# A graph network's segment sums: three written-out tiles per half and a loop of tile pairs, in place of two and a loop of single tiles

## What is computed

```
x = layernorm(x + SAGE(x))     3 layers: mean of x[src] at dst, @ Wl + bl + x @ Wr, relu between
x = layernorm(x + GIN(x))      gelu(x[src] + edge_attr @ bond_W + bond_b) * edge_weight1, summed at dst; two dense layers
x = layernorm(x + GCN(x))      2 layers: (x @ W)[src] scaled by degrees and edge_weight, summed at dst; relu, layer norm
x = layernorm(x + RGCN(x))     2 layers: h_rel[edge_type, src] summed at dst, + h @ loop_w + b
```

## Time and profile before

| what | value |
|---|---|
| median of 3 runs | 6518.18 us (6513.54 to 6526.69) |
| profiled execution | 6529.06 us |
| its span, first to last instruction | 6527.2 us |
| mean granted clock of PE | 0.864 of 2.4 GHz |
| busy: PE, DVE, ACT, POOL | 4735.7, 3273.3, 2416.2, 1918.4 us |
| chain that ended last | PE 22%, DVE 8%, issue 7%, ACT 4% of the span |

### The profile page before, as it was taken

One profiled execution on the slowest core, in us unless ns is written; L12 is line 12 of the kernel. 1 busy time (PEld: TensorE's weight loads), 2 busy tenths in 40 slices (PEclk: granted clock), 3 DMA queues, 4 the chain that ended last, 5 costly groups with the idle time before them and its releaser, 6 DMA issues. The chain is left out here.

```text
span 6527.2 us, 120714 instructions
## 1 busy us (share of the span) xinstructions
PE 4735.7 (73%) x23954; PEld 3001.6 (46%) x23955; DVE 3273.3 (50%) x10024; ACT 2416.2 (37%) x4967; POOL 1918.4 (29%) x1886
## 2 busy tenths in 40 slices
PE   5887677566868888756665776775888876777776
PEld 3553443233335555344442443433666644656552
DVE  4443343456444454456664666664444433555564
ACT  2342332344247776345542444442222221222222
POOL 5531760643033331064402433102223202222210
PEclk9998899788779999877787778887999998888887
DMA  4552663454234443244432444332333322333322
GB/s 132 176 167 95 203 204 123 143 163 155 84 95 143 142 145 126 86 135 138 135 114 78 142 133 133 124 111 73 112 102 103 108 96 80 96 92 98 92 82 83
DMA packets 429789, 789.70 MB, mean 121 GB/s; under 512 B 69303, under 2 KB 75250, under 8 KB 429716
## 3 DMA queue, kind: packets, MB, share of 16 engines
q1 hardware_dynamic: 375060, 671.58, 30.8%
q0 software_dynamic: 54656, 117.32, 7.4%
HBM read 480.10 MB, written 308.53 MB: 121 GB/s over the span
## 5 line engine op out<-in xcount | busy, mean ns | idle before, releaser
L1033 PE MATMUL p_agg<-onehot,msg 128*128 128x512 f16 (+1 forms) x2384 | 1046.1, 439 | 1028.6 <-DVE onehot L1430 624.0
L627 POOL DMA_INDIRECT raw<-node_s,src_i x980 | 962.1, 982 | 2036.3 <-DMA node_s<-o 855.5
L1430 DVE TENSOR_SCALAR onehot<-iota,dst_f,negbase 128x512 f16<-128x512 f16 (+1 forms) x2384 | 970.8, 443 | 972.8 <-PE p_agg L1035 470.7
L1035 PE MATMUL p_agg<-onehot,msg 128*128 128x512 f16 (+1 forms) x2384 | 1055.6, 443 | 0.0
L1033 PEld LDWEIGHTS p_agg<-onehot,msg 128*128 x2384 | 240.5, 101 | 1533.3 <-issue 1470.0
L1421 DVE TENSOR_TENSOR msg<-raw,msg x140 | 180.4, 1289 | 685.1 <-ACT msg L748 643.4
L1479 DVE BATCH_NORM_STATS2 stats<-v_ring 128x6 f32 (+1 forms) x1960 | 426.9, 281 | 187.0 <-ACT v_ring L826 135.1
L627 POOL DMA_INDIRECT raw<-node_x,src_i x392 | 379.4, 968 | 458.0 <-issue 445.4
L818 ACT ACTIVATE o<-v_ring,nmr,rstd 128x128 f32 (+1 forms) x1176 | 472.2, 483 | 101.5 <-DVE nmr L1495 95.1
L1408 DVE SCALAR_TENSOR_TENSOR hid<-type_in,p_wide 128x512 f32<-128x512 f32 x448 | 251.1, 616 | 321.1 <-PE p_wide L1013 235.3
L788 ACT ACTIVATE u<-p_agg,sage_bias 128x512 f32<-128x512 f32 x196 | 133.9, 683 | 703.8 <-PE p_agg L1064 703.4
(11 more groups left out here) (252 smaller groups left out, 7977.2 us busy)
## 6 DMA issues: line engine op xcount, KB each, us to landing
node_s<-o SPq DMA_DIRECT2D x392, 256.0 KB
feature<-u SPq DMA_DIRECT2D x294, 256.0 KB, 2.1
h_in<-feature SPq DMA_DIRECT2D x294, 256.0 KB
node_x<-o SPq DMA_DIRECT2D x294, 256.0 KB
res_in<-node_x SPq DMA_DIRECT2D x294, 256.0 KB, 3.2
h_in<-node_x SPq DMA_DIRECT2D x196, 256.0 KB
h_in<-node_s SPq DMA_DIRECT2D x196, 256.0 KB
h_t<-dinv_scratch SPq DMA_DIRECT2D x196, 256.0 KB, 3.8
```

Source lines behind the costliest of these rows:

```text
L627: nc.gpsimd.indirect_dma_start(out=raw[:, (e % RING) * BATCH + j, :], out_offset=None, in_=src_d, in_offset=bass.IndirectOffsetOnAxis(ap=s ...
L1033: nc.tensor.matmul(p_agg[:, a, :], tile_ap(msg, t, 0, D), oh, start=first, stop=True, skip_group_check=True)
L1035: return nc.tensor.matmul(p_agg[:, a, :], tile_ap(msg, t, D, 2 * D), oh, start=False, stop=True, skip_group_check=True)
L1430: return V.tensor_scalar(tile_ap(onehot, slot), iota[:, :], dst_f[:, bass.ds(t, 1)], negbase[:, bass.ds(it * 2 + a, 1)], ALU.subtract, ALU ...
```

## The change

`EVERY` becomes 3, so each half has three written tiles, needed or not. A turn of the loop takes `GROUP` = 2 tiles, with one wait and one signal for both, from a ring of two groups (four places). The setup counts turns of two, moves a first tile down where the last turn would pass tile 195 (with these edges no first tile moves), and has six more linked instructions.

```
-EVERY = 2
+EVERY = 3
+GROUP = 2
 MORE = 2
+GROUPS = -(-TILES // GROUP)
...
-        onehot = sb("onehot", [P, 2 * EVERY + MORE, HALF], F16)
+        onehot = sb("onehot", [P, 2 * EVERY + MORE * GROUP, HALF], F16)
...
-        def tile_of(t0, i0, i):
-            return (t0 + (i - i0) + EVERY).with_bounds(min_val=0, max_val=TILES - 1)
+        def tile_of(t0, i0, i, j):
+            return (t0 + (i - i0) * GROUP + (EVERY + j)).with_bounds(min_val=0, max_val=TILES - 1)
...
-            return ((i % MORE) + 2 * EVERY).with_bounds(min_val=2 * EVERY, max_val=2 * EVERY + MORE - 1)
+            return ((i % MORE) * GROUP + (2 * EVERY + j)).with_bounds(
+                min_val=2 * EVERY, max_val=2 * EVERY + MORE * GROUP - 1)
...
                             wait_apart(pe, rounds_s.oh_ready, i + 1)
-                            item(a, tile_of(t0, i0, i), ring_place(i), False).then_inc(rounds_s.oh_used, 1)
+                            for j in range(GROUP):
+                                last = item(a, tile_of(t0, i0, i, j), ring_place(i, j), False)
+                            last.then_inc(rounds_s.oh_used, 1)
...
-            link(V.scalar_tensor_tensor(out=n_items[g, :], in0=last1, scalar=float(-EVERY), in1=first,
+            link(V.scalar_tensor_tensor(out=some, in0=last1, scalar=float(-EVERY), in1=first,
                                         op0=ALU.add, op1=ALU.subtract))
+            link(V.tensor_scalar(o[g, 1, 0:GROUPS], colf[g, 0:GROUPS], float(GROUP), some, ALU.mult, ALU.is_lt))
+            link(V.tensor_reduce(n_items[g, :], o[g, 1, 0:GROUPS], AX.X, ALU.add))
+            link(V.tensor_scalar(some, n_items[g, :], float(-GROUP), float(TILES - EVERY), ALU.mult, ALU.add))
+            link(V.tensor_tensor(first, first, some, ALU.min))
+            link(V.tensor_scalar(last1, n_items[g, :], float(GROUP), float(EVERY), ALU.mult, ALU.add))
+            link(V.tensor_tensor(last1, last1, first, ALU.add))
...
                             dve.wait_ge(rounds_s.oh_used, i + 1)
-                            compare(ring_place(i), tile_of(t0, i0, i)).then_inc(rounds_s.oh_ready, 1)
+                            for j in range(GROUP):
+                                last = compare(ring_place(i, j), tile_of(t0, i0, i, j))
+                            last.then_inc(rounds_s.oh_ready, 1)
```

More of the change, by code:

```diff
@@ L370, in items_of, with ring_place @@
             return t0.with_bounds(min_val=0, max_val=TILES - EVERY), i0, i1
-        def tile_of(t0, i0, i):
-            return (t0 + (i - i0) + EVERY).with_bounds(min_val=0, max_val=TILES - 1)
-        def ring_place(i):
-            return ((i % MORE) + 2 * EVERY).with_bounds(min_val=2 * EVERY, max_val=2 * EVERY + MORE - 1)
+        def tile_of(t0, i0, i, j):
+            return (t0 + (i - i0) * GROUP + (EVERY + j)).with_bounds(min_val=0, max_val=TILES - 1)
+        def ring_place(i, j):
+            return ((i % MORE) * GROUP + (2 * EVERY + j)).with_bounds(
+                min_val=2 * EVERY, max_val=2 * EVERY + MORE * GROUP - 1)
         def each_batch(eng, e0, e1, body):
```

## The result

The changed kernel takes **6364.23 us** (median of 4 runs, 6357.67 to 6366.91), the kernel before beside it 6522.43. The ratio is 0.9756, 95% interval 0.9743 to 0.977: 2.4% faster, 158 us, and outside the range of 6445 to 6590. The profiled execution took 6366.74 us, its span is 6364.5.

What follows compares the result with a forecast made beforehand. PE was taken as busiest in every round but nowhere full, with 0.64 of tile work on the path. The terms, 139 - 63 - 127 + 50 + 1 = 0, gave 6518 us, no change, range 6445 to 6590.

Steps and rivals of the forecast that it cites:

- Counts, gap and setup: Signs: tile matmuls and compare each x2848; 0.56 us "issue" gap in every loop turn; setup +1 us.
- C: Longer halves of a round: single-tile loop turns become fewer two-tile turns of 1.75 us, -127 us (-158 to +19).
- Term E: Setup: six more linked DVE instructions at some 0.2 us each ahead of the list, +1 us.
- What would show it: Expected trace signs: two-tile turns 1.75 us apart, 21-tile half 18 us, last eight halves shorter, clock 0.85 to 0.88.
- rival 3: Faster by the clock: more matmuls per half raise PE's mean granted clock by 0.02, -61 us, 6457 us; chance 0.10.
- A: Third written tile on PE in the 384 halves with no turn: +139 us (bounds +68 and +227).
- D: DVE's flag to PE comes 0.32 us later, after three compares instead of two: +50 us (bounds 0 and 96).
- B: The 272 halves with one turn: their tile is now written out, saving loop overhead, -63 us (bounds -29 and -98).
- Rival 1: Slower: the third tile and later flag lie on the PE-DVE-ACT circle's path, +75 us, 6593 us; chance 0.28.
- rival 4: The two-tile loop turn saves nothing at 2.37 us, sum +146, 6664 us; two compares could leave PE waiting; chance 0.04.
- Rival 2: Faster: PE's waits for DVE swallow the added tile, share 0.3 everywhere, -72 us, 6446 us; chance 0.24.

Runs made afterwards that it cites:

- run 3: The kernel before with MORE = 4 in place of 2 (ring of four one-hots, still two written tiles and single turns): 6424.7 us, ratio 0.9865.
- run 5: The changed kernel with MORE = 1, a ring of one group (two places): 6789.85 us against 6756.4 for the kernel before on a slower chip, ratio 1.006.
- run 11: The kernel before with one more matmul, of zeros, in each loop turn: 6693.29 us against 6756.4 for the kernel before on a slower chip, ratio 0.9918.
- run 6: The changed kernel with PE leaving out the third written tile's matmuls, DVE still making its one-hot (sums wrong): 6265.12 us, ratio 0.9617.
- run 7: The changed kernel with DVE leaving out the third written compare, PE multiplying the second one-hot twice (sums wrong): 6238.29 us, ratio 0.9567.
- run 8: The changed kernel with DVE signalling after the second compare and again after the third, in all rounds: 6339.8 us, ratio 0.9725.

## Why the prediction was wrong

**Counts, gap and setup: right.** L1036, L1038 and the compare stand at x2848. The gap is there once per turn, 0.56 us, so the row was the figure to go by. The Trainium skill's smaller one (Advanced Engine Details and Errata, Control Flow Timing) would have made C even smaller. Term E was +1; the first matmul of L1036 is 1.5 us later.

**"What would show it": half wrong.** The turn of two was to be 1.75 us and is 1.59, the 21-tile half 18 and is 14.6. Each round's last eight halves are shorter, by 22 to 35 us, and RGCN 1's halves of 3.6 us take 4.0, both as said. SAGE 0, GIN and RGCN 1 were to move least and moved by 23, 41 and 25 us; the GCN rounds were to move by less than 10 us, and GCN 1 moved by 22. RGCN 1's first 82 halves together changed by under 1 us. The clock, at 0.884, left its band of 0.85 to 0.88.

**Term C is the step that failed**: "the 15 longer halves", forecast -127 us, measured -255. The half with 19 turns was priced at 6.3 us less at full clock and takes 9.1 less, those with three turns at 1.4 and take 2.3 less. Of the 255 us, 204 lie between a half's first matmul and the nodes' own part, and 51 in what comes behind. Three things were missing in it.

- *The ring.* The prediction priced turns and never the places, and read no row of DVE's waits behind PE. Two more places are worth 88 us by themselves (run 3) and 51 to 95 of the 255 in the last 16 halves; taking them back from the change costs 162 there (run 5). They let PE run through tiles that wait for it, and let DVE leave the loop sooner.
- *The turn.* 1.75 us was taken, 1.62 called the least; it is 1.59. Over the 15 turns a round behind the halves' first ones that is 0.16 x 120, some 20 us.
- *The clock.* C was mixed 73 to 27 from full and half clock, both held as they were. But with the denser loop the clock of these halves rose, and with work put into the single-tile loop's gaps it rose too (run 11). What that gave in time was not measured. In the longest half it is little: GCN 1's had full clock before and is 7.6 us shorter all the same.

The clock's mean rose by 0.02, which was **rival 3** (chance 0.10, 61 us). It was right in the clock's direction, and its "against" was wrong: it looked at PE's waits for DVE in short halves, where the clock moved little (SAGE 2 0.78 and 0.77), and not at the loop's own gaps. It was also set up as another case beside C, while both come from the same denser loop. Its 61 us are neither shown nor refuted.

**A, the third tile on PE**: forecast +139 for the halves without a turn. The work was priced rightly: from first matmul to the nodes' own part they take 212 us more, and 227 was the forecast. The share was not: leaving the tile out gives 91 us over all halves, and in those without a turn the trace is only 48 us shorter (run 6), below A's lower bound of 68. The shares were off by round: GCN 2 0.3 us, RGCN 1 33, SAGE 2 33 of 707.

**D, DVE's later flag**: forecast +50, bounds 0 and 96. Compare and flag together measure 123 us (run 7), 67 of them in GCN 2. That is more than the upper bound, but not all of it is D: in halves with a turn the kernel before made this compare too, in its loop. In those without one it is 67 us by the traces, above the forecast and inside the bounds. There, and in GCN 2 above all, the compare's own time is on DVE's path, and the prediction counted only the flag's delay, because "a loop compare already ran there": true for halves with a turn, not for the 48 without. The flag alone is worth 20 us (run 8).

**A, B and D together**: forecast +126. Shared out by halves (D's 50 over all 784), that is +164 for those without a turn, measured +126, and -46 for those with one, measured -35. The sum was near by errors that cancel, which is luck: A too high, D too low. B by itself wasn't isolated.

**Rival 1** (6593), which wanted over 0.85 of the added work on the path, and **rival 4** (the pair saves nothing) are refuted for this kernel: 212 us of added tile work made 126 of time, DVE's part included, a share of 0.6. Run 5 shows the ground of rival 4's last sentence: with one group PE does wait for two compares, 2.52 us a turn. **Rival 2** (6446) was nearest, for another reason than its own.

What stays open: how the 80 to 118 us of the pairs divide between saved gaps and clock, as no run held the clock fixed; why RGCN 1 lost 17 us with the flag in all rounds and gained 13 with it in the SAGE rounds alone; and what the slower chips' "remote" waits are.

## What to carry to other kernels

Before pricing a loop's turn, look at both engines of the ring: rows "consumer waits for producer" and "producer waits for consumer". If the producer waits (471 us here), depth is a lever by itself (88 us here); and the grouped turn paid here only with two groups. Where gaps in a loop lie between matmuls, read the granted clock along one long loop, for a change that closes gaps can raise it. What the clock is worth is then read from the time between turns at both levels (1.18 and 1.22 us here), not from PE's busy time, since at half clock the matmuls stretch into the gaps. A unit of work written out "always" is to be priced in each stage on the engine that bounds that stage: here it was free on PE and 67 us on DVE in GCN 2, and 33 us on PE and free on DVE in RGCN 1.

## What the runs showed that was not expected

- A matmul of zeros in each turn of the loop made the kernel before 0.8% faster (ratio 0.9918), with the clock of the last 16 halves of SAGE 2 at 0.95 in place of 0.70.
- The same loop turn is 1.12 us with three matmuls and 1.18 with two, at full clock.
- A turn of one tile takes 1.18 us at full clock and 1.22 at half, SAGE 2 aside, so a clock at half level costs this loop's turns next to nothing.
- The kernel before took 3.6% and 4.7% longer (6756 and 6824 in place of 6520 us) on two chips than on the others. For the one kernel traced on both kinds all of it lies outside the last 16 halves of the rounds, which agree within 0.4% (978.8 and 975.6 us).
